# Computing the k projection of a two-layer recurrent block one PSUM bank at a time, with an earlier gate on the next weight loads

## What is computed

```python
# layer 0
xn = layernorm(x)
s  = scan(log(1 - z + 1e-8), z * (xn @ Wh.T + bh)),  z = sigmoid(xn @ Wz.T + bz)
g  = silu((silu(xn @ wg.T) * (xn @ wu.T)) @ wd.T)
x  = x + s * g
# layer 1
xn = layernorm(x)
q, k, v = xn @ W_qkv.T
s  = softmax(q k.T / 32) v
xr, xk = mu_r*xn + (1-mu_r)*xn_prev,  mu_k*xn + (1-mu_k)*xn_prev   # xn_prev: one token back
k_act = square(relu(xk @ W_k.T))                 # the part that is changed
g  = silu(sigmoid(xr @ W_r.T) * (k_act @ W_v.T))
x  = x + s * g
```

## Time and profile before

| what | us |
|---|---|
| median of 3 runs | 1592.26 |
| lowest of them | 1591.34 |
| the profiled execution | 1591.23 |
| its span on the slowest core (core 1) | 1590.1 |
| spans of the 8 cores | 1576.8 to 1590.1 |
| TensorE busy, slowest core | 1286.1 (81%) |
| VectorE busy | 553.9 (35%) |
| ScalarE busy | 307.2 (19%) |

### The profile page before, as it was taken

How to read it: one execution, slowest core, us unless ns; L and a number is a source line. 1 busy time by engine, 2 the same in 40 slices (tenths; PEclk the granted TensorE clock), 3 DMA queues, 4 the chain that set the end, 5 groups by cost and what they waited for, 6 DMA issues and landing times.

```text
span 1590.1 us, 16516 instructions; the slowest of 8 cores (1576.8 to 1590.1 us)
## 1 busy us (share of the span) xinstructions
PE 1286.1 (81%) x6016; PEld 576.9 (36%) x6016; DVE 553.9 (35%) x527; ACT 307.2 (19%) x356; POOL 142.7 (9%) x236
## 2 busy tenths in 40 slices
PE   0586989999999999992445786698799878888886
PEld 0232434444444444440111332233344434444443
DVE  0624222001212064463686260033333424434443
ACT  1223211011111232331222433222200011111110
POOL 0011111011111000001000000000000101111111
PEclk9799999999999999996777999799999999999998
DMA  8433333354544556627431232532222303333322
GB/s 174 107 59 60 52 59 62 60 98 81 80 72 75 113 111 161 159 67 161 132 115 56 52 73 45 140 74 53 66 47 34 66 14 80 83 94 97 85 74 60
DMA packets 74159, 133.29 MB, mean 84 GB/s; under 512 B 23904, under 2 KB 32096, under 8 KB 72032
## 3 DMA queue, kind: packets, MB, share of 16 engines
q0 software_dynamic: 32384, 77.61, 28.0%
q1 hardware_dynamic: 33632, 42.03, 8.4%
q10 hardware_dynamic: 8064, 12.59, 2.3%
HBM read 159.47 MB, written 29.36 MB: 119 GB/s over the span
## 4 chain that ended last, share of the span: by engine, by line
PE 71%; DVE 13%; ACT 6%; DMA 4%; issue 3%; SPq 1%; DVEq 0%; ACTq 0%; POOL 0%; POOLq 0%
PE psf L347 10%; PE psf L353 9%; PE psf L939 8%; DVE BP L145 7%; PE psf L963 7%; PE psf L826 7%; PE psf L468 7%; DVE FP L145 6%; PE psf L386 5%; PE psf L438 5%; ACT BP L145 5%; PE psf L669 4%; PE psf L752 2%; PE psf L764 2%; PE psf L602 1%
## 5 line engine op out<-in xcount | busy, mean ns | idle before, releaser
L145 ACT ACTIVATE BP<-psf 128x512 bf16<-128x512 f32 (+1 forms) x192 | 128.4, 669 | 550.8 <-PE psf L353 302.7
L347 PE MATMUL psf<-BP 128*128 128x512 bf16 x768 | 186.3, 386 | 28.4 <-DVE BP L145 25.3
L145 DVE TENSOR_TENSOR BP<-BP,psf 128x512 bf16<-128x512 bf16 x96 | 66.0, 688 | 367.3 <-ACT BP L145 366.5
L353 PE MATMUL psf<-BP 128*128 128x512 bf16 x768 | 182.6, 381 | 0.0
L211 PE MATMUL psf<-BP,ones 128*128 128x512 bf16 x64 | 33.5, 523 | 118.6 <-ACT BP L145 108.6
L939 PE MATMUL psf<-BP 128*128 128x512 bf16 x512 | 121.3, 398 | 1.3 <-DVE BP L145 1.2
L347 PEld LDWEIGHTS psf<-BP 128*128 128x128 bf16 x768 | 75.2, 99 | 124.5 <-issue 38.8
L826 PE MATMUL psf<-BP 128*128 128x512 bf16 x512 | 113.3, 383 | 6.9 <-DVE BP L145 6.9
L963 PE MATMUL psf<-BP 128*128 128x512 bf16 x512 | 115.5, 385 | 2.4 <-DVE BP L145 2.4
L468 PE MATMUL psf<-BP 128*128 128x512 bf16 x512 | 111.8, 379 | 0.0
L353 PEld LDWEIGHTS psf<-BP 128*128 128x128 bf16 x768 | 75.6, 98 | 92.4 <-issue 3.2
(11 more groups left out here) (66 smaller groups left out, 1093.9 us busy)
## 6 DMA issues: line engine op xcount, KB each, us to landing
BP<-wg POOLq DMA_DIRECT2D x48, 256.0 KB, 4.2
BP<-wu POOLq DMA_DIRECT2D x48, 256.0 KB, 4.9
BP<-wd POOLq DMA_DIRECT2D x16, 768.0 KB, 8.9
FP<-xt SPq DMA_DIRECT2D x32, 256.0 KB, 7.9
FP<-xt SPq DMA_DIRECT2D x8, 1024.0 KB, 9.8
x1s<-FP SPq DMA_DIRECT2D x8, 1024.0 KB, 7.9
FP<-x1s SPq DMA_DIRECT2D x32, 256.0 KB, 6.0
FP<-x1s POOLq DMA_DIRECT2D x16, 512.0 KB, 6.6
```

What stands on the lines that cost most here:

```text
L145: ins = fn(*a, **k)
L347: te.matmul(pg, lhsT, rhs, start=(k == 0), stop=(k == NCH - 1))
L353: ins = te.matmul(pu, lhsT, rhs, start=(k == 0), stop=(k == NCH - 1))
```

## The change

- The 16 matmuls of a unit are no longer alternated between the banks. For `half` 0 the 8 matmuls into bank 2 are issued, with an increment of `s_t` at their end, and then the 8 into bank 3 for `half` 1, with another.
- The relu and the square of a half wait for that half's 8 matmuls.
- `k_relu_mark`, one mark for both banks, becomes `k_bank_free`, a mark for each bank: the matmuls into a bank wait for the relu that last read it.
- `pf_wk2` is still gated by the unit's last matmul; it stands after the scalar instructions in program order, in another engine's queue.
- `kmarks` keeps each unit's last count. `wfree` for the first v and r loads becomes the end of unit (1,6) for parity 0 and of unit (1,7) for parity 1, where it was the end of all for both.

The number of matmuls, weight loads, activations and transfers, and their shapes, stay the same.

```diff
-        k_relu_mark = 0
+        k_bank_free = {2: 0, 3: 0}
+        kmarks = {}
         kact_done = 0
 
         def k_unit(hh, o):
-            nonlocal k_relu_mark, kact_done
+            nonlocal kact_done
             par = o % 2
             wslot = A_W0 if par == 0 else A_W1
-            pu_ap = psf[:, 1024:2048]
+            rt = BP[:, (A_T0 if par == 0 else A_T1):][:, 512:1024]
+            kdst = BP[:, R0 + o * T + hh * 1024: R0 + o * T + (hh + 1) * 1024]
             wt(te, s_w[par])
             wt(te, s_v, mixm[1 if hh == 0 else 3])
-            wt(te, s_s, k_relu_mark)
             if hh == 0 and o == 0:
                 wt(te, s_s, q_bank_free[2])
                 wt(te, s_s, q_bank_free[3])
-            for k in range(NCH):
-                lhsT = BP[:, wslot + k * 128: wslot + (k + 1) * 128]
-                for sps in range(2):
-                    rhs = BP[:, R2 + k * T + hh * 1024 + sps * 512:
-                             R2 + k * T + hh * 1024 + sps * 512 + 512]
-                    ins = te.matmul(pu_ap[:, sps * 512: sps * 512 + 512], lhsT,
-                                    rhs, start=(k == 0), stop=(k == NCH - 1))
-            inc(ins, s_t)
-            kmm = s_t.n
-            pf_wk2(par, kmm)
-            rt = BP[:, (A_T0 if par == 0 else A_T1):][:, 512:1024]
-            kdst = BP[:, R0 + o * T + hh * 1024: R0 + o * T + (hh + 1) * 1024]
+            kmm = 0
             for half in range(2):
+                bank = 2 + half
+                pu = psf[:, bank * 512: bank * 512 + 512]
+                wt(te, s_s, k_bank_free[bank])
+                for k in range(NCH):
+                    lhsT = BP[:, wslot + k * 128: wslot + (k + 1) * 128]
+                    rhs = BP[:, R2 + k * T + hh * 1024 + half * 512:
+                             R2 + k * T + hh * 1024 + half * 512 + 512]
+                    ins = te.matmul(pu, lhsT, rhs, start=(k == 0),
+                                    stop=(k == NCH - 1))
+                inc(ins, s_t)
+                kmm = s_t.n
                 wt(se, s_t, kmm)
-                sx.activation(rt, pu_ap[:, half * 512:(half + 1) * 512],
-                              AF.Relu)
-                if half == 1:
-                    k_relu_mark = s_s.n
+                sx.activation(rt, pu, AF.Relu)
+                k_bank_free[bank] = s_s.n
                 wt(se, s_v, mixm[1 if hh == 0 else 3])
                 wt(se, s_sp[0 if hh == 0 else 2])
                 wt(se, s_sp[1 if hh == 0 else 3])
                 sx.activation(kdst[:, half * 512:(half + 1) * 512], rt,
                               AF.Square)
+            pf_wk2(par, kmm)
+            kmarks[(hh, o)] = kmm
             kact_done = s_s.n
...
-        wfree = {0: s_t.n, 1: s_t.n}
+        wfree = {0: kmarks[(1, 6)], 1: kmarks[(1, 7)]}
```

## The result

The changed kernel takes 1556.12 us in the median of its runs (1553.83 the lowest), the kernel before 1592.13 us. The ratio is 0.976, with a 95% interval from 0.973 to 0.979. That is 36.0 us less, where 41.3 were forecast (1551 us, range 1544 to 1562). The profiled execution has a span of 1554.7 us on its slowest core, now core 0, against 1590.1 on core 1.

What follows compares the result with a forecast made beforehand. TensorE bounds the kernel, stalled 2.31 us between k units by ScalarE's second relu. Gains of 14.6 (to C's start), 19.1 (group C), 5.2 (gate) and 2.4 (clock) sum to 41.3 us: 1551 us, range 1544 to 1562.

Steps and rivals of the forecast that it cites:

- The relu wait: Between k units: TensorE's 2.31 us stall for the second relu goes, since ScalarE needs 2.8 us per unit against 3.45.
- group C: Last k units, (1,0) to (1,7), before the v stage: length 31.0 us against 50.0, 19.1 us gained.
- The weight wait: In the k groups: a weight slot's round takes 7.90 us against 6.90 of matmuls, leaving 1.0 us idle per two units.
- The clock: In the k groups: full clock despite 1.0 us idle in 7.9, except in unit (0,0), which follows 5.37 us of idle.
- rival 2: In the k groups and v start: the clock keeps falling, + 12 us, 1563 us; chance 0.12.
- Group A: First k units, (0,0) to (0,3): done at 883.50, before 891.49; CSMM(3) behind the q block comes 8.4 us earlier.
- Groups B to C: From the second k group through the q block to the third: 14.6 us gained by C's start, 8.42 before B.
- VectorE would cap C's start: Before the last k group: VectorE's mixes(3) end at 939.39, so it starts at about 939.55, before 954.18.
- The earlier gate: Before the v stage: v and r loads issued earlier cut the idle from 7.97 to 2.8 us, another 5.2 us.
- the reloads as harmless: Before the v stage: the eight reloads come behind the first pair of loads and do not share DMA engines with it for long.
- The clock after it: First v block and a later r block: about half the low-clock loss goes, 1.7 + 0.7 = 2.4 us, bounds 0 and 4.

Runs made afterwards that it cites:

- e11: Changed kernel with own weight slots for units (1,2) to (1,7), loads paced by unit ends, v and r loads gated by (1,4) and (1,6); median 1551.0 us, ratio 0.973.
- e3: Changed kernel, but all matmuls of a unit wait for the previous unit's second relu, one mark instead of one per bank; ratio 0.988 to the kernel before.
- e6: Changed kernel with a second copy of each W_k load for units (1,2) to (1,7), issued just ahead of the real one; median 1567.9 us, ratio 0.982.
- e5: Changed kernel with own weight slots for units (1,2) to (1,7), loaded during the last q block, v and r loads gated by (1,0) and (1,1); 1556.1 us.
- e2: Changed kernel with the gate of before: first v and r loads wait for the last k matmul; 1564.8 us, ratio 0.983 to the kernel before.
- e8: Changed kernel with the gate of before and ScalarE's eight reloads held until the first v and r loads have landed; 1563.9 us, ratio 0.979.
- e9: Changed kernel with ScalarE's eight reloads held until the first v and r loads have landed; 1561.2 us, ratio 0.977 to the kernel before.
- e10: Changed kernel without ScalarE's eight reloads of the normalised input on all cores, so its output is not the reference's; 1556.0 us, ratio 0.977.

## Why the prediction was right, step by step

**The relu wait** and its replacement by the weight wait were right. In group C the loads of W_k end all of the idles on the slowest core, at every second unit, and e11 shows that with the loads out of the way the units run without a gap.

**The weight wait** was mis-sized, and it is the largest miss. I took a slot round of 7.90 us with a landing of 3.5 (3.7 for the first) and 0.25 from the landing to the matmul. The chain of waits of the changed kernel on core 0 has

```profile
948.07 3.63 PE psf L674 x16
951.70 0.02 issue
951.74 0.49 issue
952.23 4.01 DMA BP<-wk
956.24 0.35 issue
956.59 3.63 PE psf L674 x16
```

which is 8.52 us. The three rounds of group C took 8.27, 8.52 and 8.42 us on this core, where I had 8.1, 7.9 and 7.9: 1.3 us in all. Of these, 1.0 is the landing (3.76, 4.01 and 3.92 us) and 0.3 the 0.35 us from landing to matmul. In the mean of the cores the group is 1.6 us longer than forecast. The 3.5 us was the median of core 1, at the low end of the cores: over the eight cores the medians for group C's loads were 3.5 to 3.8 us before the change, with loads 6 to 7.6 us apart, 3.5 to 3.9 after it, at 3.45 and 5 us apart in turn, and 3.5 to 4.0 in e3, at 4.5 us apart. With each load doubled (e6) they were 4.4 to 5.7. So the closer spacing alone hardly shows in the medians, and twice the bytes do; why single landings were 4 us here stays open.

**The clock** in the groups was right: every unit of group C ran at full clock, on core 0 and on the seven others, and rival 2 did not occur. In the kernel before, on core 1, five of the 12 units after 2.31 us of idle ran about half of their matmuls at 1.2 GHz (5.22 to 5.30 us for 3.61), and so did unit (0,0) after 5.37; in the changed kernel the idles of up to 1.8 us between units on core 0 left it at 2.4. The timelines of all 14 profiles, from 840 to 1060 us on all cores, say the same: of the 1078 stretches of q, k, v and r matmuls that followed an idle of 0.6 to 1.92 us none was slowed, the shortest idle before a slowed one was 1.97 us (three cores of e5, 8.75 us for 7.07), and every idle above 3.7 us was followed by one. In between it went both ways. The Trainium skill ("TensorE: Matmul & The Clock Gate", section "A second HAM failure mode: psum-queue depth-cycling") tells of a kernel at 512 columns which cycles through PSUM banks and whose short idles make the clock swing. This pattern does not bear it out: group C of the changed kernel changes the bank every eighth matmul with idles of 1.20 to 1.45 us and kept a granted clock of 1.00, and e11 has 128 such matmuls without an idle in 27.79 us, the full-clock pace. What went before each fall seen here was an idle time of 1.97 us or more, whatever the banks.

**Group A** gained 7.0 us to group B and not 8.4. Two things took the rest. The start of the group's third and fourth units came later than worked out: A to the q block took 17.3 us in the mean for my 16.6. And CSMM(3) ran longer at the low clock (5.6 us for 5.05 in the mean), which undid the 0.43 us gained in the q block. Its 16 matmuls, in the busy time by window of before (core 1) and after (core 0):

```profile
911.30:916.43 5.13, 5.09 (x16) 1.98 (x17) 0.00 (x0) 0.00 (x0) 0.00 (x0) 0.67 0.01 3
```

```profile
902.30:907.77 5.47, 5.44 (x16) 2.08 (x17) 0.00 (x0) 0.00 (x0) 0.00 (x0) 0.63 0.01 3
```

**Groups B to C** came out as forecast (6.0 for 6.2). That VectorE would cap C's start was right on some cores and not on all. Where it was, this is the row (core 2 of the changed kernel):

```profile
942.04 7.07 PE L674 MATMUL psf<-BP 128*128 128x512 bf16 x31 [0.57 <-DVE BP L145]
```

On core 0 it was the q block, held 0.53 us by its own writes.

**The earlier gate** was worth 4.1 us in the mean of the cores and not 5.2. The term came from core 1, which had the longest idle of the eight (7.97 us against a mean of 6.7); the others could not gain that much. The idle left, 2.8 us, came out at 2.7 in the mean, but in part by luck. I took r's load to land after 4.8 to 4.9 us; it did so, or sooner, on four cores and took 6.4 to 7.2 on the four others. On three of those (2, 5 and 7) unit (1,7) had itself waited 1.83, 1.47 and 2.13 us, which hid the longer landing (idles of 2.0 to 3.0); on core 0 it had not, and the idle was 5.1. I had the reloads as harmless ("come behind it"); e2 with e8, and e9 with e10, show that they make most of what is long in this wait.

**The clock after it** was taken at 2.4 us and gave 1.0. My price was again core 1's (9.48 us for v's first block, the r block after it at 5.07). Over the cores v's first block went from 9.25 to 7.94 us, a gain of 1.3. The r block gave nothing: after its unchanged idle of 2.65 us it was slowed on four cores before and on five after.

So the mechanism stands, and what lies between 41.3 and 36.0 us are sizes: 1.6 in the weight round, 1.4 in group A, 1.4 in the clock after the stage, 1.1 in the gate (with B to C's 0.2 they make 5.8 in the mean of the cores, added before rounding, and the medians differ by 5.3 from the forecast). Three of the four come from taking one core, its longest wait or its quick landing, for the typical one.

## What to carry to other kernels

When a stall goes away, the loads gated by the same work move with it: work out the round (work, issue, landing, start) of each buffer slot beside the new pace, and take the landing as its range over all cores and not as one core's median. Take idle prices as means over all cores when each core has its own wait, and the slowest core's own only if it will be the slowest again. Before loads are moved earlier, look whose transfers run there: six loads in the wrong place cost as much as they saved, and the same six, paced, made the best version here.

## What had not been expected of the hardware

- A core's wait depends on where the other cores are. With the changed kernel the same load landed after 4.3 to 4.9 us on four cores and after 6.4 to 7.2 on the later core of each neighbouring pair, and left idles from 1.8 to 5.1 us; without the 4 MB of reloads per core six landings were 4.4 to 4.6 us, two 5.5 and 6.2, and the idles 1.8 to 2.9.
- A transfer that frees a staging tile can hold TensorE by way of ScalarE: q writes of 128 KB that took 1.9 us to land took 4.1 with six weight loads beside them, one of them 5.45, and stretched the way from group B to group C by some 3.8 us in the mean.
- A late load can cost more than its lateness: after idles of 3.7 to 4.1 us two units took 9.7 to 9.8 us instead of 7.07. An idle of up to 1.92 us cost no clock in any of 1078 cases; from 1.97 us on it sometimes did.
